# Loads and weight splits of the opening put in the order of use, in a fused gated-attention and expert kernel

## The reference

```
n  = layernorm(x)
q, k, v = n@Wq + bq, n@Wk + bk, n@Wv + bv             # 16 heads of 32
alpha = 0.9 * sigmoid(silu(n@Wg1 + bg1)@Wg2 + bg2) + 0.1
intra = softmax(causal(q k^T / sqrt(32))) v           # within chunks of 64 tokens
inter_t = q_t S;   S = alpha_t * S + k_t v_t^T        # a scan over all tokens
x = x + inter + intra
n  = layernorm(x)
probs = softmax(n @ router_w.T); the best 8 of 64 experts, weights normalised
x = x + sum over those experts (at most 256 tokens each) w_e * (silu(n Wg_e) * (n Wu_e)) Wd_e
      + (silu(n Wsg) * (n Wsu)) Wsd                   # a shared expert, width 384
```

## Time and profile before

| | us |
|---|---|
| three timed runs | 4373.31, 4373.85, 4375.62 |
| median | 4373.85 |
| profiled execution, its own time | 4374.81 |
| its span (first to last instruction) | 4373.1 |
| PE busy | 4239.3 |
| DVE busy | 3481.6 |
| ACT busy | 2285.9 |
| POOL busy | 1339.1 |

### The profile page before, as it was taken

The page is one execution under the profiler, slowest core; times in us unless marked ns, Lnnn a source line. Parts: engine busy times, 40 slices in busy tenths (PEclk is TensorE's granted clock), DMA queues, the critical chain, the costliest instruction groups (busy, mean ns, idle before and its releaser), DMA issues. The chain is left out here.

```text
span 4373.1 us, 182288 instructions
## 1 busy us (share of the span) xinstructions
PE 4239.3 (97%) x73868; PEld 3804.2 (87%) x73868; DVE 3481.6 (80%) x7674; ACT 2285.9 (52%) x7515; POOL 1339.1 (31%) x1266
## 2 busy tenths in 40 slices
PE   5999999999999999999999999999999599999998
PEld 4888888888888888888888888888888499999998
DVE  5878887878888778788788877787887588888887
ACT  4444555545544544455555545444454266666665
POOL 1222222222222222222222222222222266666666
PEclk9999999999999999999999999999999699999999
DMA  2111111101010110000110011011110389999997
GB/s 67 34 38 33 33 33 35 36 33 33 33 38 33 33 38 33 33 33 33 38 34 33 33 38 33 33 33 38 33 33 29 129 252 267 266 267 270 268 268 187
DMA packets 195679, 357.32 MB, mean 82 GB/s; under 512 B 17856, under 2 KB 94016, under 8 KB 194992
## 3 DMA queue, kind: packets, MB, share of 16 engines
q1 hardware_dynamic: 161488, 268.55, 18.4%
q0 software_dynamic: 33632, 79.73, 8.2%
HBM read 242.95 MB, written 107.50 MB: 80 GB/s over the span
## 5 line engine op out<-in xcount | busy, mean ns | idle before, releaser
L494 POOL TENSOR_TENSOR RI<-PV,AL 128x512 f32<-128x512 f32 x64 | 77.6, 1213 | 2562.9 <-DVE PV L1287 2562.9
L618 ACT ACTIVATE PR<-PR,MX 128x64 f32<-128x64 f32 x2048 | 680.4, 337 | 0.0
L802 PE MATMUL bank<-XBh,wsguh 128*128 128x256 f32 x1536 | 443.4, 289 | 0.0
L1936 PE MATMUL ebank<-XH,WH 128*128 128x256 f32 x1536 | 431.6, 281 | 7.0 <-DVE XL L2018 7.0
L804 PE MATMUL bank<-XBh,wsgul 128*128 128x256 f32 x1536 | 431.1, 281 | 0.0
L803 PE MATMUL bank<-XBl,wsguh 128*128 128x256 f32 x1536 | 430.8, 280 | 0.0
L1936 PE MATMUL ebank<-XH,WL 128*128 128x256 f32 x1536 | 430.1, 280 | 0.0
L1936 PE MATMUL ebank<-XL,WH 128*128 128x256 f32 x1536 | 429.9, 280 | 0.0
L618 ACT ACTIVATION_READ_ACCUMULATOR PR<-PR,MX 128x1 f32 x2048 | 389.3, 190 | 0.0
L2011 DVE TENSOR_TENSOR WL<-WS,WH 128x768 fp32r<-128x768 f32 (+1 forms) x455 | 370.4, 838 | 16.2
L626 ACT ACTIVATE OTs<-ot_bank 128x256 f32<-128x256 f32 x256 | 97.2, 380 | 517.6 <-PE ot_bank L960 517.6
(11 more groups left out here) (231 smaller groups left out, 13311.8 us busy)
## 6 DMA issues: line engine op xcount, KB each, us to landing
WS<-in_L_ffn_w_gate_dram SPq DMA_DIRECT2D x65, 768.0 KB
WS<-in_L_ffn_w_up_dram SPq DMA_DIRECT2D x65, 768.0 KB
WS<-in_L_ffn_w_down_dram SPq DMA_DIRECT2D x65, 768.0 KB
norm_rows<-XR SPq DMA_DIRECT2D x64, 576.0 KB, 3.5
X<-in_L_attn_x_dram SPq DMA_DIRECT2D x64, 512.0 KB, 3.6
out_dram<-X SPq DMA_DIRECT2D x64, 512.0 KB, 2.9
CR<-token_counts,count_at POOLq DMA_INDIRECT x136
XG<-norm_rows,row_at POOLq DMA_INDIRECT x132, 6.5
```

What stands on the lines that cost most here:

```text
L494: nc.gpsimd.tensor_tensor(inverse[:, :, 0:half], PV[:, :, :], running[:, :, HC:half:-1], ALU.mult).then_inc(folded.sem, 1)
L618: ins = nc.scalar.activation(PR[b][:, j, :], PR[b][:, j, :], ACT.Exp, bias=MX[b][:, j:j + 1], scale=1.0, accum_out=SU[b][:, j:j + 1])
L802: nc.tensor.matmul(out, sh, mh, start=first, stop=False)
L1936: last = nc.tensor.matmul(bank[HID[m]][:, a * CAP:(a + 1) * CAP], w, x[odd][:, c, :], start=(c == 0 and i == 0), stop=(c == KC - 1 and i = ...
```

## The change

- SP issues X, the router weights, Wg1, then wq0, the b1 copies, wq1, Wg2 and the other biases, wk, bv, wv, wsgu, block 1's X and wsd. It no longer waits for `begun`. Each piece has a count of its own; Wg1, the router weights, bv and the remaining small ones have one each. wsd's two pieces are staged in QT[1] and KT[1] and so wait for the split of wq1 and wk1.
- Priming is shared by ACT, PE and DVE, each a third of the events.
- POOL makes ident and neg_half first, then waits for block 0's variance, and makes the other constants after that pow. Before its loop of blocks it waits until wsgu1 is split (staged in QD).
- The splits stand between block 0's instructions on ACT and DVE, in the order of the list `SPLIT`; PE and the others wait for the count of the piece they need (`split_count`).

The diff, cut to what the text speaks of:

```diff
-        stages = [QT[0], QT[1], KT[0], KT[1], QD, KD, V, X2, KTok, AL, XN]
-        staged = []
+        STAGES = {"wq": (QT[0], QT[1]), "wk": (KT[0], KT[1]), "wv": (V, KTok), "wsgu": (X2, QD, XN), "wsd": (QT[1], KT[1])}
+        piece = {}
...
+        SMALL_DMAS = 2 * len(COPIES) + 3
+        piece_in = {name: sem(f"{name}_in") for name in piece}
+
+        SPLIT = ["wg1", "wq0", "rw", "wq1", "wg2", "wk0", "wk1", "wv0", "wv1", "wsgu0", "wsgu1", "wsgu2", "wsd0", "wsd1"]
+
+        def split_count(name):
+
+            return SPLIT.index(name) + 1
...
-            sp.wait_ge(begun, 1)
+            def load_piece(name):
+                st, _, _, src = piece[name]
+                sp.dma_start(st, src).then_inc(piece_in[name], 16)
+
             load_x(Turn(0, 0))
-            for (dst, _, _, src), come in zip(staged[:-1], piece_in):
-                sp.dma_start(dst, src).then_inc(come, 16)
+            sp.dma_start(rw, router_w).then_inc(rw_in, 16)
             sp.wait_ge(gate_clear, 1)
             for at in COPIES:
-                sp.dma_start(wg1_f[:, :, at:at + GH], Wg1.rearrange("(c p) n -> p c n", p=P)).then_inc(weights_in, 16)
-                sp.dma_start(wg2_f[at:at + GH, :], Wg2).then_inc(weights_in, 16)
-                sp.dma_start(b1[at:at + GH, :], bg1.rearrange("(p o) -> p o", o=1)).then_inc(weights_in, 16)
-            sp.dma_start(rw, router_w).then_inc(weights_in, 16)
-            for dst, src in ((bq4, bq), (bk4, bk), (b2, bg2)):
-                sp.dma_start(dst[:, :], src.rearrange("(c p) -> p c", p=P)).then_inc(weights_in, 16)
-            sp.dma_start(bvb[:, :], bv.rearrange("(o n) -> o n", o=1).to_broadcast([P, DIM])).then_inc(weights_in, 16)
+                sp.dma_start(wg1_f[:, :, at:at + GH], Wg1.rearrange("(c p) n -> p c n", p=P)).then_inc(wg1_in, 16)
+            load_piece("wq0")
+            for at in COPIES:
+                sp.dma_start(b1[at:at + GH, :], bg1.rearrange("(p o) -> p o", o=1)).then_inc(small_in, 16)
+            load_piece("wq1")
+            for at in COPIES:
+                sp.dma_start(wg2_f[at:at + GH, :], Wg2).then_inc(small_in, 16)
+            for dst, src in ((b2, bg2), (bq4, bq), (bk4, bk)):
+                sp.dma_start(dst[:, :], src.rearrange("(c p) -> p c", p=P)).then_inc(small_in, 16)
+            load_piece("wk0")
+            load_piece("wk1")
+            sp.dma_start(bvb[:, :], bv.rearrange("(o n) -> o n", o=1).to_broadcast([P, DIM])).then_inc(bvb_in, 16)
+            load_piece("wv0")
+            load_piece("wv1")
+            load_piece("wsgu0")
+            load_piece("wsgu1")
+            sp.wait_ge(xt_filled.sem, Turn(0, 0).value(xt_filled))
+            load_piece("wsgu2")
             load_x(Turn(0, 1))
+            sp.wait_ge(w_low, split_count("wq1"))
+            load_piece("wsd0")
+            sp.wait_ge(w_low, split_count("wk1"))
+            load_piece("wsd1")
...
-            for ev in primed:
-                pool.sem_inc(ev.sem, ev.early)
-            pool.sem_inc(begun, 1)
...
+            pool.sem_inc(ident_made, 1)
+            nc.gpsimd.memset(neg_half[:, :], -0.5).then_inc(half_made, 1)
+            pool.wait_ge(half_made, 1)
+
+            def rstd1(t):
+
+                pool.wait_ge(var1_ready.sem, t.value(var1_ready))
+                nc.gpsimd.tensor_tensor(rs1[:, :], ve1[:, :], neg_half[:, :], ALU.pow).then_inc(rstd1_ready.sem, 1)
+
+            rstd1(Turn(0, 0))
...
-            rstd1(Turn(0, 0))
             unpair(Turn(0, 0))
+            pool.wait_ge(w_low, split_count("wsgu1"))
...
+            for ev in primed[0::3]:
+                act.sem_inc(ev.sem, ev.early)
+
+            def piece_high(name):
+
+                st, high, _, _ = piece[name]
+                act.wait_ge(piece_in[name], 16)
+                nc.scalar.activation(high, st, ACT.Copy).then_inc(w_high, 1)
...
+                act.wait_ge(small_in, 16 * SMALL_DMAS)
...
+            gate1_high()
             normalise(Turn(0, 0))
+            piece_high("wq0")
+            router_high()
             xt_evac(Turn(0, 0), 0)
             xt_evac(Turn(0, 0), 1)
+            piece_high("wq1")
+            gate2_high()
             gate1(Turn(0, 0))
             q_evac(Turn(0, 0), 0)
             s1_high(Turn(0, 0))
+            piece_high("wk0")
+            piece_high("wk1")
             gate2(Turn(0, 0), 0)
             gate2(Turn(0, 0), 1)
             alpha(Turn(0, 0))
+            piece_high("wv0")
+            piece_high("wv1")
             k_evac(Turn(0, 0), 0)
             k_evac(Turn(0, 0), 1)
+            piece_high("wsgu0")
+            piece_high("wsgu1")
+            piece_high("wsgu2")
             q_evac(Turn(0, 0), 1)
+            piece_high("wsd0")
+            piece_high("wsd1")
             ktok_evac(Turn(0, 0), 0)
...
-            pe.wait_ge(consts_made, 1)
+            pe.wait_ge(ident_made, 1)
             pe.wait_ge(consts_done, 1)
-            pe.wait_ge(weights_in, 16 * WEIGHT_DMAS)
+            for ev in primed[1::3]:
+                pe.sem_inc(ev.sem, ev.early)
+            pe.wait_ge(rw_in, 16)
...
             xt(Turn(0, 0), 0)
             xt(Turn(0, 0), 1)
+            split("rw")
             gate1(Turn(0, 0))
+            split("wq1")
             project(Turn(0, 0), 0, wq, q_filled, ("Qa", "Qb"))
+            split("wg2")
             gate2(Turn(0, 0), 0)
             gate2(Turn(0, 0), 1)
+            split("wk1")
             project(Turn(0, 0), 0, wk, k_filled, ("Ka", "Kb"))
             project(Turn(0, 0), 1, wk, k_filled, ("Ka", "Kb"), parts=(0,))
             project(Turn(0, 0), 1, wq, q_filled, ("Qa", "Qb"), parts=(0,))
             project(Turn(0, 0), 1, wk, k_filled, ("Ka", "Kb"), parts=(1,))
+            split("wv1")
...
             scores(Turn(0, 0), 0)
+            pe.wait_ge(consts_made, 1)
             ktok(Turn(0, 0), 0)
             ktok(Turn(0, 0), 1)
             state_updates(Turn(0, 0), 0)
+            split("wsd1")
             xt(Turn(0, 1), 0)
             xt(Turn(0, 1), 1)
             state_updates(Turn(0, 0), 1)
...
             norm1(Turn(0, 0))
+            gate1_low()
             shift1(Turn(0, 0))
+            piece_low("wq0")
+            router_low()
             xt_low(Turn(0, 0), 0)
             xt_low(Turn(0, 0), 1)
+            piece_low("wq1")
+            gate2_low()
             silu1(Turn(0, 0))
             s1_low(Turn(0, 0))
+            piece_low("wk0")
+            piece_low("wk1")
+            dve.wait_ge(consts_made, 1)
             decays(Turn(0, 0))
             products(Turn(0, 0))
             inverse(Turn(0, 0), 0)
             inverse(Turn(0, 0), 1)
+            piece_low("wv0")
+            piece_low("wv1")
+            piece_low("wsgu0")
+            piece_low("wsgu1")
+            piece_low("wsgu2")
+            piece_low("wsd0")
+            piece_low("wsd1")
+            dve.wait_ge(bvb_in, 16)
             values(Turn(0, 0), 0)
             values(Turn(0, 0), 1)
```

More of the change, by code:

```diff
@@ L352, in pieces_of @@
             return [w[:, 0:chunks, i:i + TB] for i in range(0, width, TB)]
-        stages = [QT[0], QT[1], KT[0], KT[1], QD, KD, V, X2, KTok, AL, XN]
-        staged = []
-        for w, src, chunks, width in ((wq, Wq, KC, DIM), (wk, Wk, KC, DIM), (wv, Wv, KC, DIM),
-                                      (wsgu, ws_gate_up, KC, 2 * F), (wsd, ws_down, FC, DIM)):
+        STAGES = {"wq": (QT[0], QT[1]), "wk": (KT[0], KT[1]), "wv": (V, KTok), "wsgu": (X2, QD, XN), "wsd": (QT[1], KT[1])}
+        piece = {}
+        for name, w, src, chunks, width in (("wq", wq, Wq, KC, DIM), ("wk", wk, Wk, KC, DIM), ("wv", wv, Wv, KC, DIM),
+                                            ("wsgu", wsgu, ws_gate_up, KC, 2 * F), ("wsd", wsd, ws_down, FC, DIM)):
             rows = src.rearrange("(c p) n -> p c n", p=P)
             for i, (high, low) in enumerate(zip(pieces_of(w[0], chunks, width), pieces_of(w[1], chunks, width))):
-                st = stages[len(staged)]
-                st = (st[:, :, :].rearrange("p a b -> p (a b)")[:, 0:chunks * TB].rearrange("p (c n) -> p c n", c=chunks))
-                staged.append((st, high, low, rows[:, :, i * TB:(i + 1) * TB]))
+                st = (STAGES[name][i][:, :, :].rearrange("p a b -> p (a b)")[:, 0:chunks * TB]
+                      .rearrange("p (c n) -> p c n", c=chunks))
+                piece[f"{name}{i}"] = (st, high, low, rows[:, :, i * TB:(i + 1) * TB])
         wg2_f = OTs[0][:, :, :].rearrange("p a b -> p (a b)")
@@ L657, in gu, with gate1_high, router_high, gate2_high @@
                 nc.scalar.activation(TG[:, :], bank_of(f"GU{m}")[:, 0:TB], ACT.Tanh, scale=0.5).then_inc(gu_tanh.sem, 1)
[L659 to L671, removed]
+            for ev in primed[0::3]:
[4 more added lines that the diff above has]
+                nc.scalar.activation(high, st, ACT.Copy).then_inc(w_high, 1)
+            def gate1_high():
+                act.wait_ge(wg1_in, 16 * len(COPIES))
```

(45 more changed lines are left out.)

20 lines of the change are left out of this document (8 added, 12 removed).

## The result

| | before | after |
|---|---|---|
| median of the timed runs | 4374.30 (8 runs, 4371.29 to 4379.41) | 4362.15 (8 runs, 4358.07 to 4366.88) |
| profiled execution, its own time | 4374.81 | 4365.76 |
| its span | 4373.1 | 4364.0 |

The ratio is 0.9975 [0.9966, 0.9984]: 12.2 us faster, where 21 were forecast, and 3.2 us above the range.

What follows compares the result with a forecast made beforehand. PE was taken to bound the kernel, its loop running a fixed time from entry. Terms -30.96 + 0.6 + 0.4 + 1.0 + 8.0 = -21.0 us from 4374.8, less 1.0 to the median, gave 4353 us; range 4346 to 4359.

Steps and rivals of the forecast that it cites:

- Earlier X: Opening: SP issues X at 0.75 us, so block 0's statistics start at 4.5 instead of 35.46, -30.96 us.
- Loads: Opening: Wg1 and the small loads land in time, cost nothing; a late first Wg1 load would cost +3 us.
- Rival C: Opening: first loads come late through a slow queue or Wg1's 64-byte pieces; 4356 to 4360, taken as 4358 us; 13%.
- wg1's low beside the pow: Block 0's opening: DVE's low part of wg1 may not overlap POOL's pow; +0.6 us, between 0 and 0.7.
- wq0 and router before xt's lows: Block 0, norm to second low part: wq0's and the router's splitting now stands there; +0.4 us, bounds 0 and 1.6.
- wk0, wk1 on alpha: Block 0, before gate2's tanh: two high parts on ACT exceed its 1.04 us idle time; +1.0 us on alpha.
- Seven lows: Block 0, reciprocals to values: DVE's wv, wsgu, wsd lows take turns with POOL products; +8.0 us, lower bound +2.35.
- P: Experiments' theory for the opening: the lows on DVE take turns with POOL's products at one port.
- rival B: Opening: no port conflict, lows and long POOL products overlap, +2.35 for +8.0 and 0 for 0.6; 4347 us; 19%.
- Clock: First two blocks: PE now stops three times; how its clock falls can shift the end 2 us either way.
- Rival A: Opening: PE never regains the upper clock, 26.8 us of work at half clock; 4380 us; 3%.
- Rival D: Token loop: it gives the lead back because something else sets its entry; 4373 us, no change; 2%.

Runs made afterwards that it cites:

- e3_late: Changed kernel with 22 memsets of RI on POOL before block 0's pow, delaying block 0, PE's list untouched; 4380.07 us, ratio 1.0014 to the kernel before.
- f3_before_early: Kernel before the change, only without SP's wait for POOL's priming before its loads; 4365.44 us, ratio 0.9987 to the kernel before.
- e2_pool_primes: Changed kernel with PE's third of the priming counts handed out by POOL instead; 4355.15 us, ratio 0.9957 to the kernel before.

## Why the prediction was wrong

The step that failed is the one that stands first: "Nothing there waits for loads, so that loop runs for a fixed time from whenever it is entered". From whenever it is entered is right: e3_late entered it 19.2 us later and ended 19.0 later, f3_before_early 5.9 earlier and ended 6.3 earlier. The fixed time is wrong, because the change moved the loop's code. The same loop took 3256.0 us behind 480 instructions and 3265.7 behind 505; 25 idle semaphore instructions alone cost the old kernel 10.0 us. The prediction put the instructions added to PE's list at nothing without a word: it prices the priming on DVE in time, and not that PE's share lengthens the list in front of PE's loop. (It also counts 61 events and 20 for DVE. The traces have 71 and 23, which at 6.0 us for 71 is the same 2.0 us.) The sign by which the forecast called itself wrong as a whole, a loop differing by over 3 us, came true: from the first scores to the end it is 4316.2 against 4300.8, 15.5 more in this pair of traces, of which 9.7 lie between block 1 and 63.

The stops were in the trace of before: 2.13 us without a releaser at the first jump. The earlier trace rows said 3236.7 of 3250 us busy, and I read the missing 13 us as nothing.

The steps of the opening, against the difference between the traces:

- *Earlier X*: -30.96 predicted, -30.91 measured (4.55 against 35.46).
- *Loads*: nothing predicted. The high part of wg1 is at 6.11, its low ends at 7.46, before norm at 7.57. Rival C is out.
- *wg1's low beside the pow*: +0.6 predicted, 0 measured. The pow takes 0.74 beside the low's 0.69, neither waits.
- *wq0 and router before xt's lows*: +0.4 predicted. The first gate matmul comes 5.40 us after norm, where it was 5.20: +0.2.
- *wk0, wk1 on alpha*: +1.0 predicted. ACT did copy them in front of the tanh (20.11 to 22.11), but q's matmuls, which come earlier, took 1.0 us less than in the old kernel (24 matmuls busy for 3.04 us in the second row below, 4.00 in the first). That was luck. PEclk says 1.00 for both rows, but the matmuls themselves start 0.21 us apart up to 49.3 in before and 0.12 apart behind it; in after the step comes at 16.3. 0.21 is the distance that such matmuls have where PEclk is 0.50 (the gate matmuls of the next block, 59.94 to 61.85 in after), so it was the clock that rose sooner after the first gate matmul. So 14 of q's 24 matmuls ran at the slow pace before and 4 after. The prediction gave the clock 2 us either way and didn't look for it here. Together, tanh is 31.01 earlier: the steps up to here cost nothing instead of 2.0.

Stretches of PE with q's matmuls, of before, then of after:

```profile
46.80:50.90 4.10, 4.00 (x24) 3.79 (x23) 0.51 (x2) 0.86 (x3) 0.00 (x0) 1.00 0.00 0
```

```profile
16.00:19.10 3.10, 3.04 (x24) 2.84 (x23) 0.51 (x2) 0.82 (x3) 0.00 (x0) 1.00 1.01 308
```

Where the pace changes, before, then after:

```profile
49.08 0.41 PE L802 MATMUL bank<-XTh,wqh 128*128 128x256 f32 x1
49.29 0.33 PE L803 MATMUL bank<-XTl,wqh 128*128 128x256 f32 x1
49.46 0.28 PE L804 MATMUL bank<-XTh,wql 128*128 128x256 f32 x1
```

```profile
16.09 0.41 PE L857 MATMUL bank<-XTh,wql 128*128 128x256 f32 x1
16.31 0.39 PE L855 MATMUL bank<-XTh,wqh 128*128 128x256 f32 x1
16.52 0.29 PE L856 MATMUL bank<-XTl,wqh 128*128 128x256 f32 x1
```

- *Seven lows*: +8.0 predicted. From the end of the reciprocals to POOL's last product it is 15.95 us, before it was 9.53: **+6.4**, of which 2.5 is POOL's wait for wsgu1's low and the rest its longer instructions. With lows that read nothing it was 11.9, +2.4, about the lower bound I gave (2.35). So P is right, rival B is wrong, and the upper bound was too high: POOL's last two products, 4.5 us, ran when the last low (end 42.08) was over.
- *Last product near 51*: it ended at 47.72, 24.5 earlier instead of 21.2.
- *Clock*: up to 2 us either way predicted, 1.6 us lost from there to block 1, where after has 23.3 us at half clock from its first scores on and before 14.6. Rival A, 26.8 us at half clock, didn't come.
- *Rival D*, that the loop gives the lead back: it named the right place, and some 10 of 22.9 us went there, but not its mechanism. e3_late shows that the entry has no part in it.

The opening was thus worth more than I said, 22.9 us at block 1, and 23.4 and 23.6 us by time where the code lies alike. The two errors have opposite signs: 2 us too little for the opening, some 10 us not seen in the loop. At the code's old place but for 2 instructions (e2_pool_primes), the change gives -19.4 us.

At the port the prediction set the Trainium skill (SBUF — State Buffer, "Who interferes with whom") beside its price of 8.0. That section calls the shared pair of ports an exclusive lock. The rows of the long products agree (1.95 and 2.22 against 1.20 where the lows read nothing), those of the pow beside wg1's low don't: 0.74 and 0.69 overlap from 6.77 to 7.33, and neither is longer than alone.

What stays open. That PE runs dry because its instructions arrive too late is read from the packets of the queue "instruction" that stand in front of every stop; the trace doesn't name the engine that a packet is for, and no run changed the packets themselves. Most of them stop nothing (some 527 packets in the loop, and 2 to 16 stops), and why just these do isn't shown beyond that they stand at the jumps and at small matmuls. Nor is it known which place is best. The waits on issue grew by 6.3 us and the loop by 9.7; the other 3.4 are in PE's busy time, spread over blocks whose median rose from 52.20 to 52.27, and were not traced.

## What to carry to other kernels

Count an edit's instructions on each engine, not only their time: on an engine that is the bound and runs a long unrolled loop, what stands ahead of the loop moves its code, and here that was worth 10 us either way, half of the change. Before you judge a change of a few tenths of a per cent, look at the steps of the lead block by block and at the idle time put down to "issue", and compare it with the old kernel padded to the same number of instructions. Fewer instructions are not the aim: taking the priming off PE gave back 6 us, and 42 idle instructions more on PE gave back 11.5. Where so little is at stake, a few paddings have to be tried.

## What the runs showed of the hardware

- PE stops for 1.5 to 3.0 us at the jump of a loop of this size, in front of the first run of 32x32 matmuls behind it or within it, once or twice according to where the code lies. Behind such a stop the clock falls to 1.2 GHz for some microseconds (0.66 and 0.67 in the mean of 10 us).
- Each of 114 stops on "issue" in 13 traces ends 2.2 to 3.3 us after a packet of 16 KB on the queue "instruction" began (17% by chance), and the kernels with the long loop fetch one packet more, 545 against 544.
- The stop within the first 32 small matmuls moved from after 28 to after 27 and 16 small matmuls with 2 and 25 instructions more ahead of the loop.
- 25 semaphore instructions on PE, run while it waits, cost 10.0 us; 67 cost -1.5, within what can be told from nothing.
- A low part on DVE and a product on POOL that would take 1.2 us each take 1.95 to 2.25 each when they meet; a product of 16 columns takes 0.99 instead of 0.24.
- What a program runs after its loop took 1015.4 and 1019.8 us in two traces of one kernel: a single pair of traces can't settle 4 us.
